# P.V as three narrow passes into one set of 66 columns in an attention and feed-forward layer on one Trainium2 core

## What is computed

```python
kv_up = _rms_norm(kv_c, kv_norm_w) @ wkv_b.T
k_nope, v = (kv_up[..., :QK_NOPE], kv_up[..., QK_NOPE:])
scores = (einsum('bshd,bthd->bhst', q_nope, k_nope)
          + einsum('bshd,btd->bhst', q_pe, k_pe)) * scale
probs = softmax(where(causal, scores, finfo.min), axis=-1)
out = einsum('bhst,bthd->bshd', probs, v).reshape(b, s, NH * V_DIM)
return out @ wo.T
```

## Time and profile before

| what | value |
|---|---|
| median of three executions | 1614.83 us |
| span of the profiled execution, first to last instruction | 1608.3 us |
| TensorE (PE) busy | 1528.2 us, 95% |
| ScalarE (ACT) busy | 1121.8 us, 70% |
| VectorE (DVE) busy | 1103.5 us, 69% |
| GpSimd (POOL) busy | 954.8 us, 59% |
| TensorE's granted clock, mean over the span | 0.989 of full speed |

### The profile page before, as it was taken

How to read it: one execution, slowest core, us unless ns; L and a number is a source line. 1 busy time by engine, 2 the same in 40 slices (tenths; PEclk the granted TensorE clock), 3 DMA queues, 4 the chain that set the end, 5 groups by cost and what they waited for, 6 DMA issues and landing times.

```text
span 1608.3 us, 30457 instructions
## 1 busy us (share of the span) xinstructions
PE 1528.2 (95%) x10720; PEld 1278.0 (79%) x10720; DVE 1103.5 (69%) x2509; ACT 1121.8 (70%) x2207; POOL 954.8 (59%) x913
## 2 busy tenths in 40 slices
PE   6978999999999999999999999999978999999997
PEld 5866788888788888887888888888866778888875
DVE  6976777888787778887788888888875332323344
ACT  5777888878888887887888888888866553221144
POOL 2666867778677777776877878778722221111134
PEclk9999999999999999999999999999998999999999
DMA  8779999999999999999999999999988001101022
GB/s 278 258 164 209 189 209 194 207 210 185 205 191 205 187 205 204 189 212 202 186 198 193 184 197 184 200 193 186 190 220 294 27 27 40 40 1 41 1 79 105
DMA packets 661096, 268.85 MB, mean 167 GB/s; under 512 B 608432, under 2 KB 619184, under 8 KB 658768
## 3 DMA queue, kind: packets, MB, share of 16 engines
q1 hardware_dynamic: 660944, 266.90, 78.8%
HBM read 69.70 MB, written 29.36 MB: 62 GB/s over the span
## 4 chain that ended last, share of the span: by engine, by line
PE 73%; DMA 7%; DVE 6%; POOL 5%; ACT 4%; SPq 3%; issue 3%; POOLq 0%; ACTq 0%; DVEq 0%
PE s_ps L1076 20%; PE x_ps L163 16%; PE f_ps L163 13%; PE o_ps L1090 12%; PE fd_ps L163 6%; DMA qs<-q_raw 5%; PE x_ps L1099 1%; POOL qf L1680 1%; SPq L877 1%; POOL qs L1677 1%; POOL q_low L1687 1%; DMA pt<-pk 1%; PE x_ps L1107 1%; PE f_ps L1034 1%; PE a_ps L163 1%
## 5 line engine op out<-in xcount | busy, mean ns | idle before, releaser
L1521 DVE SCALAR_TENSOR_TENSOR pk<-s_ps,pk 128x512 f16<-128x512 f32 (+7 forms) x512 | 380.7, 752 | 119.1 <-ACT pk L1293 117.8
L1285 ACT ACTIVATE s_ps<-s_ps,nbias 128x512 f32<-128x512 f32 (+7 forms) x512 | 364.6, 719 | 61.7 <-DVE nbias L1508 57.7
L1508 DVE CUSTOM_DVE_ANT_0 s_ps<-s_ps,far_sb 128x512 f32<-128x512 f32 (+7 forms) x512 | 385.7, 761 | 29.2 <-PE s_ps L1076 28.4
L1293 ACT ACTIVATE pk<-s_ps 128x512 f16<-128x512 f32 (+7 forms) x512 | 327.3, 655 | 19.5 <-DMA pt<-pk 11.2
L1090 PEld LDWEIGHTS o_ps<-lat,pt 128*128 128x128 f16 x4608 | 266.7, 97 | 66.4 <-issue 61.5
L1090 PE MATMUL o_ps<-lat,pt 128*128 128x130 f16 x4608 | 307.9, 220 | 9.0 <-ACT o_norm L1302 6.4
L1076 PE MATMUL s_ps<-k_high,q_high 128*128 128x512 f32 (+3 forms) x768 | 285.2, 371 | 17.6 <-POOL q_low L1687 9.4
L1677 POOL TENSOR_TENSOR qs<-qs,sin_q 64x512 f32<-64x512 f32 x128 | 164.4, 1285 | 185.4 <-DMA qs<-q_raw 180.1
L1076 PE MATMUL s_ps<-k_low,q_high 128*128 128x512 f32 (+3 forms) x768 | 257.3, 342 | 0.0
L1718 POOL TENSOR_TENSOR mid_low<-mid,mid_high 128x512 fp32r<-128x512 f32 (+1 forms) x44 | 56.8, 1290 | 296.5 <-ACT mid_high L1382 296.5
L1076 PE MATMUL s_ps<-k_high,q_low 128*128 128x512 f32 (+3 forms) x768 | 220.8, 341 | 0.0
(11 more groups left out here) (142 smaller groups left out, 2614.1 us busy)
## 6 DMA issues: line engine op xcount, KB each, us to landing
weff_in<-weff SPq DMA_DIRECT2D x64, 256.0 KB, 3.4
qs<-q_raw SPq DMA_DIRECT2D x256, 64.0 KB, 2.6
weff<-weff_sb SPq DMA_DIRECT2D x8, 1024.0 KB, 5.3
wo_sb<-wo SPq DMA_DIRECT2D x16, 512.0 KB, 4.9
m_fold<-m_in SPq DMA_DIRECT2D x8, 1024.0 KB, 7.4
m_in<-m_fold SPq DMA_DIRECT2D x8, 1024.0 KB, 6.4
xin<-x SPq DMA_DIRECT2D x16, 256.0 KB, 4.4
wqn_sb<-wqn SPq DMA_DIRECT2D x8, 512.0 KB, 6.1
```

The source lines that it names most:

```text
L1285: e.activation(M.scores_of(i), M.scores_of(i), ACT.Exp, bias=M.nbias[:, i % 4:i % 4 + 1], scale=-1.0).then_inc(S.exp)
L1293: e.activation(M.halves_of(i)[:, :, 0, :], M.tiles_of(i), ACT.Copy, scale=P_SCALE).then_inc(S.p_high)
L1508: e.tensor_tensor_reduce(out=s, in0=s, in1=M.far_sb[:, SEQ - width:SEQ], scale=1.0, scalar=3e38, op0=ALU.add, op1=ALU.min, accum_out=M.nbi ...
L1521: e.scalar_tensor_tensor(out=M.halves_of(i)[:, :, 1, :], in0=M.tiles_of(i), scalar=P_SCALE, in1=M.halves_of(i)[:, :, 0, :], op0=ALU.mult, ...
```

## The change

`values` makes three passes for each key tile instead of two: the high half of the probabilities with 66 columns (the latents' high half and the ones), the high half again with the 64 columns of the latents' low half, and the low half with the first 66 columns. All three accumulate into the same 66 columns of `o_ps`. The product of the two low halves, which was computed before, is left out. `outputs_norm` then has 64 columns per job and writes them straight into `o_pair`; it waits for `outputs_turn` of two heads earlier, since `o_pair` has no second buffer. `outputs_add` and `o_norm` are gone. `lat2` has the ones between its halves. Many steps of the tables have other values.

```diff
-    minimum=(0.2, -0.65, -0.54, -0.43, -0.89, 0.17, 0.39, -0.15),
-    exponential=(1.8, 0.94, 2.11, 1.54, 0.93, 1.31, 0.42, 1.74),
-    split_high=(3.32, 2.37, 2.26, 1.81, 1.16, 1.4, 1.57, 1.74),
-    split_low=(1.8, 2.01, 2.83, 2.1, 2.29, 1.58, 1.57, 0.74),
+    minimum=(0.18, -0.43, -0.53, -1.09, -0.8, 0.18, 0.29, -0.32),
+    exponential=(1.8, 0.8, 2.11, 1.54, 1.5, 1.13, 0.42, 1.68),
+    split_high=(2.98, 2.29, 2.26, 1.81, 1.99, 1.42, 1.47, 1.86),
+    split_low=(1.54, 0.84, 2.99, 2.46, 2.29, 1.58, 1.57, 0.79),
 PAIR_STEPS = dict(
-    invert_sums=(6.57, 6.96, 9.0, 8.51),
-    turn_probs=(3.93, 3.01, 3.47, 2.28),
-    values=(7.55, 8.84, 8.32, 8.66),
-    outputs_norm=(8.34, 9.63, 9.4, 8.31),
+    invert_sums=(6.57, 8.78, 9.05, 8.53),
+    turn_probs=(4.67, 4.14, 2.26, 2.29),
+    values=(7.58, 8.87, 8.28, 8.91),
+    outputs_norm=(8.25, 9.54, 9.31, 8.3),
-CHUNK_STEPS = dict(
-    outputs_add=(17.23, 13.26),
 ROW_STEPS = dict(
-    outputs_turn=(14.44, 14.03),
-    outputs_high=(14.77, 14.72),
-    outputs_low=(13.72, 14.63),
+    outputs_turn=(13.89, 14.1),
+    outputs_high=(14.42, 14.83),
+    outputs_low=(14.24, 14.57),
 QUERY_STEPS = dict(
-    queries=(0.41, 3.67),
-    queries_raw=(0.17, 3.99),
-    queries_swap=(0.99, 4.79),
-    queries_turn=(4.43, 6.88),
+    queries=(0.44, 3.62),
+    queries_raw=(0.61, 3.75),
+    queries_swap=(1.02, 4.84),
+    queries_turn=(2.91, 4.77),
...
-QUERIES_LOAD, OUTPUT_LOAD, FOLD_STORE = 3.9, 42.47, 4.28
-VALUES_LOAD = (4.38, 1.66)
+QUERIES_LOAD, OUTPUT_LOAD, FOLD_STORE = 3.96, 43.01, 4.31
+VALUES_LOAD = (2.72, 5.68)
...
-END_STEP, END_EVERY = 16.49, 3.75
+END_STEP, END_EVERY = 15.52, 3.75
-EARLY_START, EARLY_EVERY = 6.3, 1.66
+EARLY_START, EARLY_EVERY = 6.17, 1.66
...
+SUMW = KVL + 2
...
-        self.o_ps = o_ps[:, 0:2 * LATW].rearrange("p (u d) -> p u d", u=2)
+        self.o_ps = o_ps[:, 0:2 * SUMW].rearrange("p (u d) -> p u d", u=2)
...
-            blocks = range(2 * PAIR)[blocks_of(i)]
-            for m in blocks:
-                ins = e.matmul(M.o_ps[:, i % 2, :], M.pt[:, u % NPT, m, :],
-                               M.lat2[:, b * JT + (m - blocks[0]) // 2, :], start=m == blocks[0],
-                               stop=m == blocks[-1])
+            blocks = blocks_of(i)
+            tiles = (blocks.stop - blocks.start) // 2
+            for t in range(tiles):
+                high, low = (M.pt[:, u % NPT, blocks.start + 2 * t + h, :] for h in range(2))
+                lat = M.lat2[:, b * JT + t, :]
+                e.matmul(M.o_ps[:, i % 2, :], high, lat[:, 0:SUMW], start=t == 0, stop=False)
+                e.matmul(M.o_ps[:, i % 2, 0:KVL], high, lat[:, SUMW:LATW], start=False, stop=False)
+                ins = e.matmul(M.o_ps[:, i % 2, :], low, lat[:, 0:SUMW], start=False,
+                               stop=t == tiles - 1)
         ins.then_inc(S.pv)
 
     def outputs_turn(p, c):
-        w.wait_ge(S.o_add, 2 * (2 * p + 1) + c + 1)
+        w.wait_ge(S.o_norm, 4 * (2 * p + 1) + 2 * c + 2)
...
     def outputs_norm(u):
+        n, c = u // 4, u // 2 % 2
+        cols = slice(n % 2 * KVL, (n % 2 + 1) * KVL)
         w.wait_ge(S.rinv, u + 1)
-        if 2 * u >= NON:
-            w.wait_ge(S.o_add, (2 * u - NON) // 4 + 1)
+        if n >= 2:
+            w.wait_ge(S.ot_mm, 2 * (n // 2 - 1) + c + 1)
         for side in range(2):
             r = (2 * u + side) % NON
-            ins = e.activation(M.o_norm[:, r, :], M.o_ps[:, side, 0:P], ACT.Copy,
-                               scale=M.rinv[:, r:r + 1])
+            ins = e.activation(M.o_pair[:, c, u % 2 * 2 + side, cols], M.o_ps[:, side, 0:KVL],
+                               ACT.Copy, scale=M.rinv[:, r:r + 1])
         ins.then_inc(S.o_norm)
...
-    def outputs_add(k):
...
-        e.tensor_tensor(M.o_pair[:, c, :, side], M.o_norm[:, r:r + 4, 0:KVL],
-                        M.o_norm[:, r:r + 4, KVL:P], ALU.add).then_inc(S.o_add)
```

More of the change, by code:

```diff
@@ L49 @@
 )
 PAIR_STEPS = dict(
-    invert_sums=(6.57, 6.96, 9.0, 8.51),
-    turn_probs=(3.93, 3.01, 3.47, 2.28),
-    values=(7.55, 8.84, 8.32, 8.66),
-    outputs_norm=(8.34, 9.63, 9.4, 8.31),
-)
-CHUNK_STEPS = dict(
-    outputs_add=(17.23, 13.26),
+    invert_sums=(6.57, 8.78, 9.05, 8.53),
+    turn_probs=(4.67, 4.14, 2.26, 2.29),
+    values=(7.58, 8.87, 8.28, 8.91),
+    outputs_norm=(8.25, 9.54, 9.31, 8.3),
 )
 ROW_STEPS = dict(
-    outputs_turn=(14.44, 14.03),
-    outputs_high=(14.77, 14.72),
-    outputs_low=(13.72, 14.63),
+    outputs_turn=(13.89, 14.1),
@@ L66 @@
+    outputs_high=(14.42, 14.83),
+    outputs_low=(14.24, 14.57),
 )
 QUERY_STEPS = dict(
-    queries=(0.41, 3.67),
-    queries_raw=(0.17, 3.99),
-    queries_swap=(0.99, 4.79),
-    queries_turn=(4.43, 6.88),
+    queries=(0.44, 3.62),
+    queries_raw=(0.61, 3.75),
+    queries_swap=(1.02, 4.84),
+    queries_turn=(2.91, 4.77),
 )
 OUTPUT_STEPS = dict(
-    output=(12.54, 15.27, 20.32, 23.55, 28.43, 31.29, 36.73, 39.63),
-    output_add=(12.8, 15.24, 21.4, 22.74, 28.63, 31.17, 38.24, 39.21),
+    output=(12.96, 15.39, 20.63, 23.8, 28.58, 31.65, 36.22, 39.88),
@@ L78 @@
+    output_add=(12.54, 15.18, 21.82, 22.86, 28.63, 31.17, 38.1, 39.2),
 )
 FOLD_STEPS = dict(
-    fold_values=(1.03, 0.88),
-    fold_high=(1.03, 1.23),
-    fold_low=(1.43, 0.19),
-)
-QUERIES_LOAD, OUTPUT_LOAD, FOLD_STORE = 3.9, 42.47, 4.28
-VALUES_LOAD = (4.38, 1.66)
-OUTPUT_STORE = (19.03, 23.94, 27.18, 28.69, 34.27, 37.19, 39.5, 47.47, 1.5)
-LAST_OUTPUT = dict(output=(0.0,), output_add=(1.26,))
-END_STEP, END_EVERY = 16.49, 3.75
+    fold_values=(1.03, 0.71),
+    fold_high=(1.56, 1.22),
+    fold_low=(1.39, -0.28),
+)
@@ L93 @@
+QUERIES_LOAD, OUTPUT_LOAD, FOLD_STORE = 3.96, 43.01, 4.31
+VALUES_LOAD = (2.72, 5.68)
+OUTPUT_STORE = (20.37, 27.8, 28.9, 35.68, 34.93, 38.36, 38.08, 47.13, 1.72)
+LAST_OUTPUT = dict(
+    output=(0.25,),
+    output_add=(1.39,),
+)
+END_STEP, END_EVERY = 15.52, 3.75
 AFTER_TILE = dict(x_load=-2.13, statistics=-0.35, deviation=-0.05, normalise=0.81, transpose_x=1.12,
@@ L219, in __init__ @@
             new(n) for n in ("pv_mm", "rinv_done", "o_normed"))
-        self.o_add, self.ot_mm, self.ot_high, self.ot_low = (
-            new(n) for n in ("o_added", "o_transposed", "ot_high", "ot_low"))
+        self.ot_mm, self.ot_high, self.ot_low = (
+            new(n) for n in ("o_transposed", "ot_high", "ot_low"))
         self.wv_in, self.wo_in, self.m_in, self.m_out = (
@@ L382, in attention @@
         self.pt = sb(ctx, "pt", [P, NPT, 2 * PAIR, P], F16)
-        self.o_norm = sb(ctx, "o_norm", [P, NON, P])
         self.o_pair = sb(ctx, "o_pair", [P, 2, 4, P])
@@ L514, in attention_order @@
     for k in range(NJ // 4):
-        then(4 * k + 3, CHUNK_STEPS, k % 2, k)
         if k // 2 % 2:
@@ L1516, in invert_sums @@
             w.wait_ge(S.o_norm, u - NON // 2 + 1)
-        e.reciprocal(M.rinv[:, r:r + 2], M.o_ps[:, :, P]).then_inc(S.rinv)
+        e.reciprocal(M.rinv[:, r:r + 2], M.o_ps[:, :, KVL]).then_inc(S.rinv)
     def split_low(i):
@@ L1644, in latents_begin @@
                         base=0, pattern=[[-1, P]], channel_multiplier=1).then_inc(S.ident)
-        e.memset(M.lat2[:, :, P:LATW], 1.0).then_inc(S.ident)
+        e.memset(M.lat2[:, :, KVL:SUMW], 1.0).then_inc(S.ident)
     def halves(i):
@@ L1652, in halves @@
         w.wait_ge(S.lat_high, i + 1)
-        e.tensor_tensor(M.lat2[:, i, KVL:P], M.kl[:, r, :], M.lat2[:, i, 0:KVL], ALU.subtract
+        e.tensor_tensor(M.lat2[:, i, SUMW:LATW], M.kl[:, r, :], M.lat2[:, i, 0:KVL], ALU.subtract
                         ).then_inc(S.lat)
@@ L1695, in latents_over @@
             w.wait_ge(S.weff_out[r], DMA * STEPS // 2)
-    def outputs_add(k):
[L1698 to L1703, removed]
-        e.tensor_tensor(M.o_pair[:, c, :, side], M.o_norm[:, r:r + 4, 0:KVL],
-                        M.o_norm[:, r:r + 4, KVL:P], ALU.add).then_inc(S.o_add)
-        last[:] = S.o_add, k + 1
     def attention_over():
@@ L1737, in gpsimd_program @@
     run(dict(latents_begin=latents_begin, halves=halves, rotary=rotary,
-             queries_turn=queries_turn, latents_over=latents_over, outputs_add=outputs_add,
+             queries_turn=queries_turn, latents_over=latents_over,
              attention_over=attention_over, residual=residual, gate_up=gate_up, finish=finish))
```

## The result

Measured: 1608.54 us median of 20 executions (1604.07 to 1613.05) against 1614.36 of 20 before (1607.35 to 1619.74); ratio 0.9971, interval 0.9960 to 0.9982. By the ratio that is 4.7 us (the two medians differ by 5.8), where 26 were forecast, and inside the range. The direction holds; the size does not, and it is only just clear of the 3 us that the prediction calls indistinguishable from none. The profiled execution has a span of 1604.7 us.

What follows compares the result with a forecast made beforehand. TensorE was taken to bound attention, with the SP queue next: P.V's saving of 56 us stops at 26, so 1608.3 - 26 = 1582.3 us of span, and the median, 6.5 above, is 1588.8 us; range 1555 to 1613.

Steps and rivals of the forecast that it cites:

- case A: Forecast case: narrow passes near 30 ns, SP queue with its DMA engines takes over; 1589 us, range 1573 to 1605, chance 0.54.
- D: Rival: SP queue and swap are already the wall, a delayed swap holding the next head's scores; 1612 to 1618, chance 0.08.
- Passes: TensorE's P.V in attention: 27 narrower passes per pair take 0.83 us for 1.05, 56 us less over all (51 to 61).
- C: Rival: P.V's weight load no longer hides, slower from 39 ns a pass on; 1633 at half unhidden, 1702 at all; chance 0.13.
- ScalarE and GpSimd: Attention: ScalarE loses 17 to 25 us, GpSimd 94 us; 0 on the path, paying indirectly through room for GpSimd's query chain.
- The added wait: ScalarE's `outputs_norm` waiting for `outputs_turn` of the two heads before, 64 times: 0 on the path, at most 64 us.
- The moved steps: Tables of steps: transpositions, value loads, swaps and query rotation at other steps cost 0, bounded by -5 and +5 us.
- Where the saving stops: SP queue in attention: it has 34 us to give for TensorE's 56, keeps 8 idle, so the gain is 26 us.
- B: Rival: SP queue is no wall, its transposition times partly backlog, and TensorE stays the bound; 1559, chance 0.20.

Runs made afterwards that it cites:

- e12: The kernel before with the swap DMAs of the queries and GpSimd's wait for them left out; ratio 0.9905 to the kernel before.
- e7: The changed kernel with a second buffer of `o_pair`, so `outputs_norm` waits for the turn of four heads earlier; ratio 0.9978 to the kernel before.
- e5: The changed kernel with the old tables of steps, those of the kernel before; ratio 1.0003 to the kernel before.
- e1: The changed kernel without the pass of high half by latents' low half, 18 passes per pair for 27; ratio 0.9929 to the kernel before.
- e2: The changed kernel with a fourth pass of 64 columns per key tile into unread columns, 36 passes per pair; ratio 1.0148 to the kernel before.
- e10: The changed kernel with the swap DMAs of the queries and GpSimd's wait for them left out; ratio 0.9717 to the kernel before.
- e9: The changed kernel with swap DMAs that carry 64 of 512 columns, as many DMAs as ever; ratio 0.9869 to the kernel before.
- e8: The changed kernel with the swap DMAs issued from ScalarE's queue instead of SP's, first swap a step later; ratio 1.0259 to the kernel before.
- e13: The changed kernel with loads of query, value and output weights issued from GpSimd's queue instead of SP's; ratio 1.0227 to the kernel before.
- e14: The changed kernel with swap DMAs issued from GpSimd's queue instead of SP's, first swap and one `queries_turn` later; ratio 1.0618 to the kernel before.

## Why the prediction was wrong in size

Two walls stand at almost the same height. Seen as a square (gain against the kernel before, in us):

| | full DMA work | 16 of 18 blocks | no swaps |
|---|---|---|---|
| kernel before | 0 | 14 | 15 |
| changed kernel | 5 | 36 | 46 |

Each relief alone brings 5 or 14 to 15; together they bring 36 and 46, about twice the sums of 19 and 20. This shows that the change relieves something real and that the queue's DMAs with the waits for them hold it back: it is worth 22 us with 16 blocks and 30 without swaps, and 5 with the full work. The lower row of the square is the whole change, new steps and GpSimd's missing addition included. That TensorE is the part that pays rests on the chain of e12. It is case A's mechanism, though at 1608.5 the time lies outside A's own 1573 to 1605, between A and D. That it still lies in the overall range is owed to the room left for other rivals. The forecast's steps fare as follows.

- **Passes.** Right within a few us: 0.84 us for the pair shown, for 0.83, and no load stands in the way, as the first two loads 20 ns apart had suggested. C's break-even of 39 ns was not near. The price of before, 1.05 us, came from a single slow pair; by the median of all pairs the saving is 48 us, below the stated 51 to 61.
- **ScalarE and GpSimd.** L1306 measures 314 ns (318 by the slope), and 94 us of GpSimd work are gone. "They pay indirectly" is not borne out: GpSimd's wait for the swap grew by 76 us and took most of the room.
- **The added wait.** Right, 0 on the path (e7).
- **The moved steps.** Wrong. Set at 0; e5 shows them at about 5 us, without which the change gains nothing that can be measured. The bound of 5 us held, only just.
- **Where the saving stops.** This is the step that failed: it set the SP queue's own work, 66.6 us per four heads, as fixed, and let the saving stop only where the queue's pauses end. 26 us were to be had so, and 5 came. The pauses themselves were sized about right: 37.8 us over all heads for the forecast's 34, of which 22 went for the forecast's 26. What the forecast had at nothing is that the queue's rows and short gaps would grow, and they grew by 15 us: 7.3 in the swaps' rows, 3.8 in the transpositions', 3.8 in short gaps. The kernel before has one such trace only. The growth goes with the number of TensorE's passes (e1, e2), and its cause stays open. The 34 also holds some luck: the 22 gaps of the earlier trace rows are not all 0.08 to 0.10 us. Three are 0.36, 0.50 and 1.78 us, and one merged row hides a pause of 1.4 us, so this stretch had 4.0 us of pauses, not 2.1, more than the other heads.
- **D**, the queue and the swap already at the wall, with 1612 to 1618, was nearer to the result than A's 1589. Its evidence against, TensorE busy for 97.5%, was no evidence, as both can be nearly full at once; the chain from 300 to 900 us had shown the swap in it.
- **B** falls with e1: with TensorE's load down by a further 70 us (0.554 us per pair by the median in place of 0.827) the time falls by 7.

Not settled: how the 25 us of e10 over e9 split between SP's issue and the chain from swap to rotation to scores, which is a bound of its own kind, since it is a delay and not a full queue; why the queue's rows grow with TensorE's passes; and what the new steps are worth where the queue is relieved. e8, e13 and e14 change other engines' queues too, so they show that moving the issue doesn't pay, but don't price it alone.

## What to carry to other kernels

When the busiest engine is at 97% look for a second resource that is equally full, DMA queues above all, since a queue that issues is not counted as busy and its waits look like waits for data. Read the chain over the whole phase, not over one good stretch. Don't take a saving from a queue's idle time with its work held fixed: here the rows of the same DMAs grew by more than half of what the pauses gave. Add up the rows instead of multiplying a median. To test for two walls at one height, lighten each on both kernels: gains that more than add up mean that both stand.

## What was not expected of the hardware

- Passes of 64 to 66 columns in float16, each with its own load of 128x128 weights, follow one another every 30 to 31 ns, three in a row into the same columns of the accumulator, with no sign of a stall.
- A transposition's time on the SP queue is not fixed. Its mean over the 256 is 3.12 us before and 3.13 after, 2.94 in the kernel before without swaps (e12) but 3.17 in the changed one without them (e10), 3.04 with light swaps (e9), and 3.36 and 3.28 with transfers from a second queue (e13, e8). With the passes of TensorE alone it goes from 3.11 (18, e1) over 3.13 (27) to 3.18 (36, e2).
- The mean granted clock in attention was lower where TensorE idled more: 1.00 before (26 us idle of 1060), 0.99 after (51), 0.98 with two passes (e1, 91). 1.00 is the 2.4 GHz level.
- A DMA issued from ScalarE holds that engine: 256 issues of 0.60 us by the median in e8, with 66 us of ScalarE's instructions waiting behind them, and none such in the changed kernel.
